# Four attention and feed-forward stages of a two-layer decoder in two barrier-free programs, and ALiBi's bias added by TensorE

## The chip, the cores and the metric

The kernel runs on one core of a Trainium2 chip. The metric is the device time of one execution in microseconds, as the median of several runs. TensorE, VectorE, ScalarE, GpSimd and SyncE are called PE, DVE, ACT, POOL and SP, as in the profile. Each engine works through its own instructions in order. They meet through semaphores: an instruction waits until a count is reached, and adds to another when it is done.

## The reference

The input x has 2048 tokens (32 sequences of 64) of 256 numbers, which is 16 tiles of 128 tokens. Six parts follow each other, each added to x, and each works on the layer norm of x:

```
x = x + attention(norm(x))            # 16 heads of 128, 4-bit weights with scales, softmax over 64 keys
x = x + cross_attention(norm(x), ctx) # 16 heads of 128, 4 key heads, RMS norm, rotary, 64 context + 64 causal keys
x = x + feed_forward(norm(x))         # silu(x Wg) * (x Wu), 2 of every 4 kept, then Wd
x = x + alibi_attention(norm(x))      # 16 heads of 16, 4 key heads
x = x + channel_attention(norm(x), ctx)
x = x + experts(norm(x))              # 32 experts, top 8
```

In the ALiBi attention the logits are `q k / 4 + slope * (key - query)`, and minus infinity where the key lies behind the query; then comes the softmax, the product with v and the output projection.

## The kernel before, in words

x stays in SBUF as 16 tiles of [128 tokens, 256]. A step is four tiles. The work is written as four stages. The first three are a block of five engine programs each (`with nc.Block()`), the fourth is made of three: ALiBi, channel attention and experts, which `together` (L131) writes one after the other into each engine's program without a barrier between them. `core.stage()` (L107) ends each stage with a barrier of all engines (L112).

**The first attention** (`attn_stage`, L299) goes through 64 units, one for each step and head. The loop over n = 0 to 68 (70 on DVE) is written out: PE takes the scores of unit n-1, the projections of unit n, the transposes and the mix of unit n-3 and the output projection of unit n-4. The last four units run out without new projections behind them. L572 adds the result to x, and `measure` (L209) takes the statistics of a tile.

**The cross attention** (`cross_stage`, L667) goes in 16 units a step (4 tiles, 4 key heads), with a lag for every operation (L698): tile s is normalised at t = 4s, turned at 2 units later (L776), projected from 4 later on (keys or values, then queries, into two PSUM banks), and the scores come 11 later. ACT squares what was projected, DVE multiplies it with the rotary tables (L950, L952, L953) and sums the squares (L970). The queries of a unit go to PE only when DVE has read the last ones. `settle` (L212) stands ahead of it: it aggregates the statistics of the tiles (L218) and takes the inverse root in twelve small dependent instructions (L197 to L203, one helper for all stages). `make_tables` makes the tables at t = 1.

**Feed-forward** (`ffn_stage`, L1083) has 32 units; the down projection follows nine units behind (FFN_LAG), so PE takes the last ones with nothing else to do. For a unit, DVE keeps two of four (L1167), ACT rounds to 16 bits (L1261), POOL takes the rest (L1113), and PE multiplies (L257). L1173 adds to x. SP has nothing to do in it.

**ALiBi** (`alibi_stage`, L1687) has two units a tile (`ALIBI_PAIRS`), with the lags of L1708: turn 1 (L1769), projection 2 (L257, 24 small matmuls; ACT copies q, v in four pieces, L1844, and k in eight, L1850), scores 4 (L1795), softmax sums 5, transposes of the probabilities and mix 7, output 8. For a unit's scores DVE does three things over [128, 512]: L1890 multiplies by the scale, adds the bias and writes to SBUF; L1894 takes the largest; L1896 subtracts it. The next scores wait for L1890, as there is one PSUM bank for them. DVE's rest of the projection's input (L1900) comes behind the odd unit's L1896, and PE's projection of the next tile waits for it. Ahead of it all, POOL sets the channel attention's buffers to constants (L1925, L1599 to L1603), DVE settles all 16 tiles and clears v (L1869).

`steps` (L235) writes the first, the last and the draining pass of a body out and runs those between in a register loop. The weights of each stage come by SP in turn with what POOL has split, during the stage ahead.

Of the kernel before, what the change touches and what calls it, by code (L numbers as in the profile page):

```python
# [47 lines left out]
AT_ATTN, AT_CROSS, AT_FFN = (26 * KB, 125 * KB), (56 * KB, 157 * KB), (56 * KB, 125 * KB)  # L48
# [67 lines left out]
class Programs:  # L116
# [7 lines left out]
    ahead: Any = None  # L124

# [109 lines left out]
def steps(engine, body, unrolled=0):  # L235

    body(0, lambda k: k >= 0)
# [33 lines left out]
ATTN_BLOCK = 32  # L273

# [24 lines left out]
def attn_stage(core, w, jobs=(), first=0):  # L299
# [3 lines left out]
    region = Region(core, AT_ATTN)  # L303
    sb = lambda shape, dt=F32: region.take(shape, dt)
    bias, bo = sb([P, 3, ATTN_HEADS]), sb([P, D])
    xT = [sb([P, STEPS, KD, TOK], F16) for p in range(2)]
    xnorm = sb([P, SUBS, D])
    codes, scales = (sb([P, ATTN_RAWS, CHUNK]) for _ in range(2))
    qT, kT = (sb([P, 2, TOK]) for _ in range(2))
    v = [sb([P, 2, SUBS, ATTN_GROUP * ATTN_HD], F16) for p in range(2)]  # L310
# [21 lines left out]
    LATE = 3  # L332

# [18 lines left out]
    with nc.Block() as block:  # L352
        @block.sync
        def _(sp):
            for j, (src, sc, dst) in enumerate(raw):
                if j >= ATTN_RAWS:
                    sp.wait_ge(s_made, j - ATTN_RAWS + 1)
                to, ts = (q[:, j % ATTN_RAWS, 0:int(np.prod(src.shape[1:]))] for q in (codes, scales))
                if len(src.shape) == 3:
                    to, ts = (q.rearrange("p (t d) -> p t d", d=D) for q in (to, ts))  # L360
                sp.dma_start(to, src).then_inc(s_raw[j % ATTN_RAWS], 16)
                for b in range(P // ATTN_BLOCK):
                    sp.dma_start(ts[b * ATTN_BLOCK:(b + 1) * ATTN_BLOCK], sc[b].partition_broadcast(ATTN_BLOCK)).then_inc(s_raw[j % ATTN_RAWS], 16)
            stage_weights(core, sp, jobs, first)

        @block.tensor
        def _(pe):
            def turn_x(tile, out):
                pe.wait_ge(s_normed, tile + 1)
                for k in range(KD):  # L370
                    last = nc.tensor.transpose(out[:, k].rearrange("p b c -> p (b c)"), xnorm[:, tile % SUBS, k * P:(k + 1) * P], core.ident)
                last.then_inc(s_turned, 1)

            def project_v(u):
                i, h = head(u)
                g, j, b = h // ATTN_GROUP, h % SUBS // 2, h % 2
                if i == 0 and h % ATTN_GROUP == 0:
                    pe.wait_ge(s_made, ATTN_PER_GROUP * g + 2)
                if h == 0:
                    pe.wait_ge(s_lo, SUBS * (i + 1))  # L380
                after(pe, q_kept, u)
                for k in range(KD):
                    tokens = [q[:, i, k, (2 * j + b) * P:(2 * j + b + 1) * P] for q in xT]
                    last = product(nc, ps[:, RING[3 * u % 2], :], tokens, [w.qkv[:, ATTN_V, k, g * ATTN_GROUP * ATTN_HD:(g + 1) * ATTN_GROUP * ATTN_HD]], k == 0, k == KD - 1)
                last.then_inc(v_ready, 1)

            def project_qk(u, c, bank, ready):
                i, h = head(u)
                if i == 0 and h % ATTN_GROUP == 0:
                    pe.wait_ge(s_made, ATTN_PER_GROUP * (h // ATTN_GROUP) + (4 if c == ATTN_Q else 6))  # L390
                for k in range(KD):
# [2097 lines left out]
```

## Time and profile before

| what | value |
|---|---|
| median of 3 runs | 1947.57 us (1943.87 to 1948.71) |
| the profiled execution's own time | 1948.45 us |
| its span, first to last instruction | 1946.7 us |
| mean granted TensorE clock | 0.962 of full speed |
| busy: PE, DVE, ACT, POOL | 87%, 78%, 53%, 37% |
| first attention | 0 to 359 us |
| cross attention | 360 to 843 us |
| feed-forward | 844 to 1007 us |
| ALiBi, up to its last addition to x | 1008 to 1182 us |
| channel attention and experts | to the end |

A line of the timeline gives the start, the time, the engine, the line of the kernel, the operation, the tiles and shapes, how many instructions were merged, and in brackets the idle time before it with what ended it. The granted clock is a share of TensorE's full 2.4 GHz; 0.5 is its lower level, 1.2 GHz.

### The profile page before, as it was taken

To read this page: it belongs to the slowest core of one execution; us is meant where nothing else is said; L and a number is where in the kernel's file an instruction comes from. 1 tells how busy PE (TensorE), PEld (TensorE's weight loads), DVE (VectorE), ACT (ScalarE), POOL (GpSimd) and SP (SyncE) were. 2 spreads that over 40 slices of the span, in tenths; PEclk is the share of its full clock that TensorE was granted. 3 is DMA by queue.
4 is the path that set the end of the run, shared out by engine and by line. 5 is a ranking of instruction groups with operands and counts; after the bars stand their busy time and mean duration, and the time that the engine had idled before them with its cause. 6 is when DMAs were issued, how large, how long until landed. Compare 5 with 4: busy or idle time off the path is not lost. (4 is left out here: it accounts for less than half of the span.)

```text
span 1946.7 us, 43266 instructions
## 1 busy us (share of the span) xinstructions
PE 1694.7 (87%) x15744; PEld 1000.1 (51%) x15744; DVE 1514.0 (78%) x2893; ACT 1031.5 (53%) x2056; POOL 716.1 (37%) x941
## 2 busy tenths in 40 slices
PE   5999999589999999979946775777777889999998
PEld 2656665357777677845533442222222346656565
DVE  5766666689989898859876989999999478666654
ACT  2666666245555555534415764888888533323222
POOL 4644321487767766503352343454441000000000
PEclk9999999889999999989977997999999999999999
DMA  9601000100000000000002111333331013212121
GB/s 241 176 24 53 26 13 2 56 20 12 12 10 11 10 8 4 2 1 1 1 9 49 41 36 37 88 96 92 95 85 40 23 62 100 84 59 81 63 82 49
DMA packets 87661, 94.90 MB, mean 49 GB/s; under 512 B 17568, under 2 KB 63264, under 8 KB 87456
## 3 DMA queue, kind: packets, MB, share of 16 engines
q1 hardware_dynamic: 83712, 87.76, 15.8%
q10 hardware_dynamic: 2976, 2.32, 0.5%
q8 instruction: 127, 2.08, 0.4%
q0 software_dynamic: 768, 2.10, 0.4%
q14 instruction: 78, 0.64, 0.1%
HBM read 78.51 MB, written 10.22 MB: 46 GB/s over the span
## 5 line engine op out<-in xcount | busy, mean ns | idle before, releaser
L257 PE MATMUL ps<-arena 128*128 128x512 f16 (+6 forms) x6464 | 1094.6, 325 | 57.4 <-DVE arena L1900 13.9
L257 PEld LDWEIGHTS ps<-arena 128*128 128x128 f16 (+1 forms) x6464 | 604.9, 100 | 446.9 <-issue 43.4
L1533 ACT ACTIVATE arena<-ps 128x512 f32<-128x512 f32 x512 | 278.6, 598 | 72.3 <-PE ps L1465 49.6
L1547 DVE TENSOR_REDUCE arena<-ps 128x4 f32<-128x1024 f32 x256 | 305.3, 1218 | 11.1 <-PE ps L1457 11.0
L1513 PE MATMUL ps<-arena 128*32 128x256 f32 x2048 | 164.2, 393 | 2.8 <-ACT arena L1542 0.6
L1457 PE MATMUL ps<-arena 31*128 31x256 f16 x1024 | 102.6, 276 | 73.2 <-ACT arena L1533 52.2
L2356 DVE TENSOR_TENSOR arena<-ps,arena 128x512 f32<-128x512 f32 x96 | 66.1, 689 | 128.2 <-ACT arena L2248 111.3
L2248 ACT ACTIVATE arena<-ps 128x512 f32<-128x512 f32 x96 | 57.1, 596 | 178.8 <-PE ps L257 178.6
L1457 PEld LDWEIGHTS ps<-arena 31*128 31x128 f16 x1024 | 34.8, 92 | 188.3 <-DVE arena L1547 153.2
L1020 POOL TENSOR_TENSOR arena<-arena 128x512 f32<-128x512 f32 x96 | 98.8, 1043 | 44.7 <-DVE arena L203 43.7
L623 POOL TENSOR_TENSOR arena<-arena 128x256 f32<-128x256 f32 x64 | 39.3, 614 | 188.6 <-DVE arena L593 188.6
L486 ACT ACTIVATE arena<-ps,arena 128x512 f32<-128x512 f32 x64 | 44.0, 688 | 115.2 <-PE ps L257 115.2
L1465 PE MATMUL ps<-arena 32*128 32x256 f16 x1024 | 101.2, 276 | 0.9 <-ACT arena L1533 0.2
L2238 ACT ACTIVATE arena<-arena 128x512 f16<-128x512 f32 x96 | 60.1, 626 | 74.2 <-DVE arena L2362 73.9
L1113 POOL TENSOR_TENSOR arena<-arena 128x512 f16<-128x512 f32 x32 | 50.2, 1577 | 115.7 <-ACT arena L1261 112.4
L179 POOL TENSOR_TENSOR arena<-arena 128x256 f16<-128x256 f32 (+5 forms) x72 | 86.1, 1196 | 5.8
L886 ACT ACTIVATE arena<-ps 128x512 f16<-128x512 f32 x64 | 38.2, 597 | 82.0 <-PE ps L812 82.0
L177 POOL CAST arena<-arena 128x256 f16<-128x256 f32 (+5 forms) x72 | 45.5, 632 | 97.2 <-DMA arena<-in_L_ffn_gate_up_proj 69.0
L1034 POOL TENSOR_TENSOR arena<-arena 128x256 f32<-128x256 f32 x80 | 58.3, 728 | 60.9 <-DVE arena L953 60.8
L1025 POOL TENSOR_TENSOR arena<-arena 128x512 f32<-128x512 f32 x64 | 67.2, 1051 | 28.0 <-DVE arena L988 27.8
L952 DVE TENSOR_TENSOR arena<-ps,arena 128x512 f32<-128x512 f32 x80 | 54.9, 686 | 28.7 <-ACT arena L881 25.8
L541 DVE TENSOR_TENSOR arena<-ps,arena 128x512 f16<-128x512 f32 x64 | 43.9, 686 | 40.5 <-ACT arena L475 40.5
(199 smaller groups left out, 2919.7 us busy)
## 6 DMA issues: line engine op xcount, KB each, us to landing
arena<-moe_cw SPq DMA_DIRECT2D x64, 192.0 KB, 2.7
arena<-moe_cw SPq DMA_DIRECT2D x64, 128.0 KB, 2.9
arena<-in_L_ffn_gate_up_proj SPq DMA_DIRECT2D x16, 384.0 KB, 3.4
ch_out<-arena SPq DMA_DIRECT2D x32, 128.0 KB
arena<-moe_cw SPq DMA_DIRECT2D x64, 64.0 KB, 2.7
ch_keys<-arena SPq DMA_DIRECT2D x48, 64.0 KB, 2.0
arena<-ch_keys SPq DMA_DIRECT2D x64, 48.0 KB
arena<-arena SPq DMA_DIRECT2D x192, 16.0 KB
```

Of the source, the lines that this page charges most:

```text
L179: nc.gpsimd.tensor_tensor(lo, raw, hi, ALU.subtract).then_inc(core.s_split, 1)
L257: last = nc.tensor.matmul(out, a, b, start=start and n == 0, stop=stop and n == len(pairs) - 1, skip_group_check=not group)
L1020: nc.gpsimd.tensor_tensor(a4, a4, spread(rms[:, s % 2, u * CROSS_KVH:(u + 1) * CROSS_KVH], CROSS_HD), ALU.mult).then_inc(scaled.sem, 1)
L1025: nc.gpsimd.tensor_tensor(prob[:, k % 2], e[:, k % 2], spread(inv[:, k % 2, :], CROSS_KEYS), ALU.mult).then_inc(probs.sem, 1)
L1034: nc.gpsimd.tensor_tensor(a4[:, :, 0:half], a4[:, :, 0:half], b4[:, :, half:CROSS_HD], ALU.add)
L1457: last = nc.tensor.matmul(ps[:, bank(user) + n, u * D:(u + 1) * D], qp[rows, tile % CH_RING, set8, u * P:(u + 1) * P], kp[rows, tile % CH_ ...
L1465: last = nc.tensor.matmul(ps[:, T[(t * CH_RGS + g) % len(T)], u * D:(u + 1) * D], kp[rows, tile % CH_RING, set8, u * P:(u + 1) * P], qp[ro ...
L1513: last = nc.tensor.matmul(ps[32 * g:32 * (g + 1), O, 0:D], vz[:, half % 2, u, g, j, :], pT[:, c % 3, g, u, :], start=j == 0 and u == 0, st ...
L1533: nc.scalar.activation(pT[:, b % 3, g], ps[:, T[n % len(T)], :].rearrange("p (u t) -> p u t", u=KD), ACT.Exp, scale=CH_SCALE).then_inc(s_e ...
L1547: nc.vector.tensor_reduce(m[:, half % 2, 2 * half_pair:2 * half_pair + 2, j, :], ps[:, bank(user):bank(user) + 2, :].rearrange("p g (u s) ...
L2238: nc.scalar.activation(hT[0][:, b % 4, :], h[b % MOE_HELD], ACT.Copy).then_inc(s_hi, 1)
L2356: nc.vector.tensor_tensor(h[n % MOE_HELD], ps[:, U[n % 2], :], silu[:, n % 2, :], ALU.mult).then_inc(s_gated, 1)
```

## The change

The four stages become two, each one program: both first attentions, and feed-forward to experts. The parts that change:

- The cross attention's first six units (t = 0 to 5) are issued by PE, ACT and DVE at the end of the first attention's n = 62 to 67; its POOL program starts behind the attention's own, and its first two context loads and all credits to semaphores are issued at the very start. DVE settles tiles 0 to 11 at n = 60, and 12 to 15 behind its last statistics. The buffers are placed anew so that both fit.
- ALiBi's first four units (t = 0 to 3) are issued in feed-forward's e = 37 to 40: on PE ahead of the down projection of e, on ACT ahead of e's roundings, on DVE at the end of e. DVE settles tiles 0 to 11 at e = 37, 12 to 15 at the end. PE's first mix waits for feed-forward's last addition. SP's ALiBi loads and POOL's preparations (`open_gpsimd`) come at feed-forward's start.
- ALiBi's bias, divided into three bf16 parts, is written into the scores' bank by three matmuls with the identity, and the scores are accumulated onto it. There are two banks for the scores; k and v share one. The scale goes into ACT's copy of q. L1890 is gone; L1894 and L1896 read PSUM. e lies where the logits are, so L1896 waits for the probabilities two units back.
- POOL's constants are set in pieces: the 8192 columns of L1925 in 8, one in each unit of the first step, the rest in 13 in the next two steps. The channel attention's keys are loaded at context tile 9, not 3.
- The channel attention's first turned scores also wait for ALiBi's last addition (`keys.accumulated`), at step 13, not 16.

```diff
-        with core.stage():
-            attn_stage(core, attn, later[0], first[0])
-        with core.stage():
-            cross_stage(core, cross, later[1], first[1])
-        with core.stage():
-            ffn_stage(core, ffn)
+            second = cross_stage(core, cross, later[1], first[1])
+            together(core, attn_stage(core, attn, second, later[0], first[0]), second)
...
+            last.append(ffn_stage(core, ffn, last[2]))
             together(core, *reversed(last))
...
+ATTN_CROSS = tuple(range(ATTN_UNITS - 2, ATTN_UNITS + 4))
+FFN_ALIBI = (37, 38, 39, 40)
...
+            if n in ATTN_CROSS:
+                ahead.tensor(pe, 0, ahead.begun, ATTN_CROSS.index(n), ATTN_CROSS.index(n) + 1)
...
+            if n == ATTN_CROSS[0] - 2:
+                settle(core, dve, "x_first", 0, range(TILES - SUBS))
+            if n in ATTN_CROSS:
+                ahead.vector(dve, 0, ahead.begun, ATTN_CROSS.index(n), ATTN_CROSS.index(n) + 1)
+        settle(core, dve, "x_last", 0, range(TILES - SUBS, TILES))
...
+            if e == FFN_ALIBI[0]:
+                settle(core, dve, "al_first", 2, range(TILES - SUBS))
+            if e in FFN_ALIBI:
+                ahead.vector(dve, 0, ahead.begun, FFN_ALIBI.index(e), FFN_ALIBI.index(e) + 1)
+        settle(core, dve, "al_last", 2, range(TILES - SUBS, TILES))
...
+                pe.wait_ge(s_bias, 2 * ALIBI_PARTS)
+                pe.wait_ge(shifted.sem, shifted.at(i, k - 1))
+                for n in range(ALIBI_PARTS):
+                    nc.tensor.matmul(ps[:, SC[k % 2], :].rearrange("p (r n) -> p r n", r=2), ident[:, :], parts[:, n, :].unsqueeze(1).broadcast_to([P, 2, ALIBI_KVH * S]),
+                                     start=n == 0, stop=False, skip_group_check=True)
                 for b in range(2):
-                        last = nc.tensor.matmul(ps[b * S:(b + 1) * S, SC, :], qT[:, s % 2, a, b * S:(b + 1) * S],
-                                                kT[:, s % 2, b].rearrange("p h k -> p (h k)"), start=True, stop=True)
+                    last = nc.tensor.matmul(ps[b * S:(b + 1) * S, SC[k % 2], :], qT[:, s % 2, a, b * S:(b + 1) * S],
+                                            kT[:, s % 2, b].rearrange("p h k -> p (h k)"), start=False, stop=True, skip_group_check=True)
...
-                    dve.wait_ge(exped.sem, exped.at(i, k - 1))
-                    nc.vector.scalar_tensor_tensor(out=lg.rearrange("p (r g) k -> p r (g k)", r=2), in0=ps[:, SC, :].rearrange("p (r n) -> p r n", r=2),
...
-                    nc.vector.tensor_reduce(top[:, k % 2, :], lg, AX.X, ALU.max).then_inc(maxed.sem, 1)
+                nc.vector.tensor_reduce(top[:, k % 2, :], sc, AX.X, ALU.max).then_inc(maxed.sem, 1)
                 dve.wait_ge(maxed.sem, maxed.at(i, k + 1))
-                    nc.vector.tensor_tensor(lg, lg, spread(top[:, k % 2, :], S), ALU.subtract).then_inc(shifted.sem, 1)
+                dve.wait_ge(probs.sem, probs.at(i, k - 1))
+                nc.vector.tensor_tensor(logits[:, k % 2], sc, spread(top[:, k % 2, :], S), ALU.subtract).then_inc(shifted.sem, 1)
...
+    def open_gpsimd(pool):
+        credit(pool, probs)
+        nc.gpsimd.memset(v, 0.0).then_inc(s_zero, 1)
+        pool.wait_ge(s_const, 16)
+        nc.gpsimd.tensor_copy(ident, core.ident).then_inc(s_bias, 1)
+        left = bias.rearrange("p g k -> p (g k)")
+        for n in range(ALIBI_PARTS):
+            nc.gpsimd.tensor_copy(parts[:, n, :], left).then_inc(s_bias, 1)
...
+                if i == 0:
+                    nc.gpsimd.memset(keys.rows[:, t // 2, t % 2 * CH_HALF:(t % 2 + 1) * CH_HALF], 1.0).then_inc(s_ones, 1)
+                if 1 <= i < STEPS - 1 and (i - 1) * ALIBI_UNITS + t < ALIBI_CLEARED:
+                    ahead.clear(pool, (i - 1) * ALIBI_UNITS + t)
```

## Rows read from the trace of the kernel before

**Rows 1.** The page: busy time and instructions of each engine

```profile
PE 1694.7 (87%) x15744; PEld 1000.1 (51%) x15744; DVE 1514.0 (78%) x2893; ACT 1031.5 (53%) x2056; POOL 716.1 (37%) x941
```

**Rows 2.** Busy time in four stretches (columns as in the first line, us)

```profile
core 0: us, PE busy (x) PEld busy (x) DVE busy (x) ACT busy (x) POOL busy (x), PEclk, DMA share, GB/s
0.00:50.00 50.00, 26.24 (x192) 11.50 (x192) 29.24 (x92) 15.80 (x30) 23.04 (x22) 0.97 0.99 242
...
345.00:386.60 41.60, 24.38 (x195) 12.25 (x195) 25.20 (x77) 11.52 (x21) 17.86 (x22) 0.84 0.19 58
...
997.41:1037.80 40.39, 14.93 (x105) 10.84 (x105) 19.90 (x42) 6.12 (x24) 17.77 (x14) 0.59 0.09 27
...
1147.47:1155.61 8.14, 6.17 (x81) 3.78 (x81) 7.50 (x17) 6.13 (x21) 3.27 (x5) 1.00 0.16 48
```

**Rows 3.** Timeline of ALiBi, one tile of its repeating part, PE and DVE (start us, us, ...)

```profile
1149.21 0.42 DVE L1900 TENSOR_TENSOR arena<-ps,arena 128x256 f16<-128x256 f32 x1
...
1149.69 1.35 PE L257 MATMUL ps<-arena 128*128 128x128 f16 x24 [0.59 <-DVE arena L1900]
...
1150.97 1.08 PE L1795 MATMUL ps<-arena 128*64 128x512 f32 x4
...
1152.10 0.69 DVE L1890 SCALAR_TENSOR_TENSOR arena<-ps,arena 128x512 f32<-128x512 f32 x1 [0.26 <-PE ps L1795]
...
1152.82 0.69 DVE L1894 TENSOR_REDUCE arena<-arena 128x8 f32<-128x512 f32 x1
...
1153.14 1.08 PE L1795 MATMUL ps<-arena 128*64 128x512 f32 x4
```

**Rows 4.** Timeline, ALiBi's first scores, and a weight load of the cross stage's first projection

```profile
370.46 0.15 PEld L257 LDWEIGHTS ps<-arena 128*128 128x128 f16 x1 [0.28 <-issue]
...
1035.89 1.98 PE L1795 MATMUL ps<-arena 128*64 128x512 f32 x4
```

**Rows 5.** Timeline of feed-forward, 24 matmuls of 512 columns, and its last units

```profile
866.66 5.34 PE L257 MATMUL ps<-arena 128*128 128x512 f16 x24
...
994.57 2.43 ACT L1261 ACTIVATE arena<-arena 128x512 f16<-128x512 f32 x4 [10.19 <-DVE arena L1167]
...
995.28 5.41 POOL L1113 TENSOR_TENSOR arena<-arena 128x512 f16<-128x512 f32 x4 [7.34 <-ACT arena L1261]
...
997.41 7.08 PE L257 MATMUL ps<-arena 128*128 128x256 f16 x48 [4.13 <-POOL arena L1113]
```

**Rows 6.** Timeline from feed-forward's last addition to ALiBi's third turn

```profile
1004.53 1.42 DVE L1173 TENSOR_TENSOR arena<-ps,arena 128x256 f32<-128x256 f32 x4 [7.85 <-PE ps L257]
...
1008.28 6.92 POOL L1925 MEMSET arena<- 128x8192 f16 x1 [7.59 <-POOLq L112]
...
1009.44 5.79 DVE L197 TENSOR_SCALAR arena<-arena 128x16 f32<-128x16 f32 x1
...
1030.57 2.18 ACT L1850 ACTIVATE arena<-ps,arena 128x128 f32<-128x128 f32 x8
...
1037.79 0.69 PE L1769 MATMUL ps<-arena 128*128 128x128 f32 x2
```

**Rows 7.** Timeline, first and last instruction of one settling of 8 tiles

```profile
1122.57 0.64 DVE L218 BATCH_NORM_AGGREGATE arena<-arena 128x2 f32<-128x6 f32 x8
...
1125.65 0.17 DVE L203 SCALAR_TENSOR_TENSOR arena<-arena 128x8 f32<-128x8 f32 x1
```

**Rows 8.** Timeline, from the first attention to the cross attention

```profile
329.07 0.42 DVE L578 TENSOR_TENSOR arena<-ps,arena 128x256 f16<-128x256 f32 x1 [1.07 <-ACT arena L491]
...
356.45 1.42 DVE L572 TENSOR_TENSOR arena<-ps,arena 128x256 f32<-128x256 f32 x4 [1.21 <-PE ps L257]
...
357.78 1.40 DVE L209 BATCH_NORM_STATS2 arena<-arena 128x6 f32<-128x256 f32 x4
...
366.00 0.69 PE L776 MATMUL ps<-arena 128*128 128x128 f32 x2 [9.66 <-DVE arena L226]
...
380.00 0.41 DVE L938 TENSOR_TENSOR arena<-ps,arena 128x256 f16<-128x256 f32 x1
```

More of the change, by code:

```diff
@@ L124 @@
     ahead: Any = None
+@dataclass
+class StageAhead:
+    open_tensor: Any
+    open_scalar: Any
+    open_vector: Any
+    open_gpsimd: Any
+    begun: Any
+    tensor: Any
+    scalar: Any
+    vector: Any
 def together(core, *stages):
@@ L332, in attn_stage @@
     LATE = 3
+    ahead = cross.ahead
     def late_tile(n):
@@ L350, in x_bank @@
         return ps[:, (*RING, SC, T)[tile], 0:D].rearrange("p (k b c) -> p k b c", k=KD, b=2)
[L352 to L374, printed above, removed]
@@ L375, in project_v @@
                 i, h = head(u)
-                g, j, b = h // ATTN_GROUP, h % SUBS // 2, h % 2
+                pe.wait_ge(o_lo, u + 1)
+                if h == 0:
+                    after(pe, added, SUBS * i)
                 if i == 0 and h % ATTN_GROUP == 0:
[L378 to L391, printed above, removed]
-                    last = product(nc, ps[:, bank, :], [w.qkv[:, c, k, h * ATTN_HD:(h + 1) * ATTN_HD]], [q[:, i, k, :] for q in xT], k == 0, k == KD - 1)
-                last.then_inc(ready, 1)
@@ new lines, in tensor @@
+                    pe.wait_ge(s_made, ATTN_PER_GROUP * (h // ATTN_GROUP + 1))
+                for s in range(SUBS):
+                    last = product(nc, ps[:, A[s // 2], s % 2 * D:(s % 2 + 1) * D], [q[:, u % 2, (s % 2 * 2 + s // 2) * P:(s % 2 * 2 + s // 2 + 1) * P] for q in oT],
+                                   [w.out[:, h, :]], h == 0 and s % 2 == 0, h == ATTN_HEADS - 1, group=False)
+                last.then_inc(projected, 1)
+            if n in ATTN_CROSS:
+                ahead.tensor(pe, 0, ahead.begun, ATTN_CROSS.index(n), ATTN_CROSS.index(n) + 1)
@@ new lines, in cross_stage, with sb @@
+    homes = {"in": Region(core, AT_CROSS_IN), "early": Region(core, AT_CROSS_EARLY), "rope": Region(core, AT_CROSS_ROPE),
+             "late": Region(core, AT_CROSS_LATE), "last": Region(core, AT_CROSS_LAST)}
+    home = {"cRaw": "in", "raw": "in", "maskf": "in", "ropeA": "rope", "v": "late", "kT": "late", "shift": "last", "prob": "late", "pT": "early", "qT": "early", "top": "last"}
+    def sb(name, shape, dt):
+        return homes[home.get(name, "early")].take(shape, dt)
+    xT = [sb(f"xT{p}", [P, 2, KD, P], F16) for p in range(2)]
@@ L1923, in gpsimd @@
     def gpsimd(pool):
-        credit(pool, probs)
-        nc.gpsimd.memset(keys.rows, 1.0).then_inc(s_ones, 1)
-        ahead.clear(pool)
         def split_context(n):
```

1815 lines of the change are left out of this document (932 added, 883 removed).

## The prediction

> **What bounds the kernel now.** I read the page first: PE is busy for 87% of the span and DVE for 78% [rows 1]. Both are averages over stages with other limits, so I then went through windows of 50 us, and through the timeline of the three places that the change touches. Three things are to be seen.
>
> At the two joints nobody is near its limit. From feed-forward's last down projections to the turn of ALiBi's third tile pass 40.4 us, with PE busy for 14.9 and DVE for 19.9, at a granted clock of 0.59 [rows 2]. Most of DVE's share isn't work: a settling instruction of 16 columns takes 5.79 us while POOL fills 8192 columns in 6.92 us [rows 6], where such an instruction takes 0.17 us alone [rows 7]. From the first attention's tail to the end of the cross attention's first tile pass 41.6 us, with DVE busy for 25.2 [rows 2].
>
> ALiBi in its repeating part takes 8.14 us a tile, with DVE busy for 7.50, PE for 6.17 and ACT for 6.13 [rows 2]. What closes the loop is a chain: the projection's input is ready (L1900, 1149.63), PE projects and scores until 1152.05, DVE goes through L1890, L1894, L1896 and the rest until the next L1900 has ended, 5.67 us later at 1149.63 + 8.14 [rows 2, 3].
>
> The rest (attention, cross, feed-forward, channel, experts) keeps its instructions and order, and I give it no change beyond what is named below.
>
> **ALiBi's bias.** L1890 goes, which is 0.72 us from its start to that of L1894 [rows 3], twice a tile. L1894 and L1896 stay; reading PSUM I leave them at 0.69 us, as L1890 reads it too and takes 0.69. PE gets three matmuls of 512 columns a unit. 24 such take 5.34 us, so one is 0.22 and three are 0.66 us, 1.3 us a tile, if the clock is high [rows 5]; at the low clock a weight load with its idle time, one for each matmul, has 0.43 us [rows 4].
>
> Now the chain: the even unit's three stand between projection and scores, so PE's part grows from 2.47 to 3.1 us. DVE's part of 5.67 us loses both L1890, 1.44 us. That would be 7.35 us. But the odd unit's scores, which ended 2.17 us after the even ones (1154.22 against 1152.05 [rows 3]), now end 2.8 us after them, and DVE without one L1890 would be there about 0.4 us too early. That gives 7.7 us a tile, and PE's own work, 6.17 + 1.3 = 7.5 us, lies just under it. So about 0.45 us is saved a tile, for 13 tiles 6 us. The last tiles have no projection, and there DVE is the limit: two of them save 1.44 less what PE asks, some 2 us together. I take **-8 us**. At best DVE's whole 1.44 us is saved for 15 tiles, -22 us; at worst PE takes all back, 0. Beyond 0 I don't go at the high clock, since the chain holds both edits. The new wait of L1896 for the probabilities two units back has POOL's product as its source, which ends about as L1896 would start; I give it nothing, and what stands behind it is DVE's whole queue, so up to 0.2 us a unit, 6 us, if POOL is late.
>
> **From feed-forward to ALiBi.** Gone: the barrier, the long settling, the constants ahead of everything. Before, the last addition starts at 1004.53 and the third tile's turn at 1037.79 [rows 6]. After, I follow the tail. DVE settles twelve tiles as soon as it has kept the last units. Eight tiles take 1125.82 - 1122.57 = 3.25 us, 0.64 of it for the eight aggregations [rows 7], so twelve take 3.6 and four take 2.9. It has kept the last unit shortly before ACT's last rounding ends at 997.0 [rows 5]; the settling is done at about 1000.4, and the first tile is normalised at 1000.9. PE finished unit 28 at 999.2 (a quarter of 7.08 us from 997.41 [rows 5]) and now waits 2.3 us, with three down projections behind it. ACT is worse off: it turns the first input, and then stands before q, v and k of tile 0 (k alone is 2.18 us [rows 6], the three about 3.4), all ahead of the last rounding. PE projects at about 1003.3 to 1005.5, so that rounding comes at 1009, POOL's rest (1.35 us each [rows 5]) at 1010.6, and the last down projection ends at 1012.5 and not at 1004.5. This is the price of the moved steps: 8 us later. Then come the addition and the statistics, 2.8 us, the last settling, 2.9, and a normalisation, 0.4: 1018.7. The third tile's turn is at about **1019, and not at 1037.8: -19 us**. PE has fewer gaps on the way, so I expect the high clock earlier; ALiBi's first scores took 1.98 us and not 1.08 [rows 3, 4]. I give this 2 us: **-21**. At best the tail isn't held up at all: 1004.5 + 2.8 + 2.9 + 0.4 = 1010.6, -27. At worst the moved PE and ACT steps take the low clock and their waits add, another 8 us: -12.
>
> **From first to cross attention.** Before, the moved chain of six steps runs from the first turn, 366.00, to 380.00, 14.0 us. The attention's tail from 345.0 to its addition at 356.45 is 11.5 us [rows 8]. Both are latency chains. They could overlap, but each queue holds them in one order: DVE's rope products of tile 0 stand in front of the last unit's rounding, for which PE waits with the last output projection, and behind that PE projects for step 5. So I lay them end to end. Added is the settling of twelve tiles at n = 60: 3.6 us in DVE's queue, where PE waits for L578 in every unit and DVE has 1.07 us idle ahead of it [rows 8]; PE loses 2.3 us. Then addition and statistics, 2.8, and the last settling, 2.9. 345.0 + 11.5 + 14.0 + 2.3 + 2.8 + 2.9 = 378.5, where before it was 380.0. PE and ACT run on during the last settling, and this closes some of DVE's waits in steps 6 and 7. I take **-2 us**. At best DVE stands idle nowhere from 345 to 386.6, which saves 41.6 - 25.2 = 16.4 less 2.3 and 2.9, -11. At worst the tables and the turn's round trip aren't hidden either, +6.
>
> **Small ones.** The two context loads now leave at the start, where the DMA engines are busy for 0.99 of 50 us at 242 GB/s [rows 2]: 0.26 MB are 1.1 us, and PE waits for weights there: **+1** (0 to +2). POOL's preparations for the bias run during feed-forward's first settling: seven small instructions, of which DVE may wait for some, **+1** (0 to +3). The 21 pieces of the constants in ALiBi's steps, 6.92 / 8 = 0.87 us each for the larger, can hold DVE's normalisation, once a tile; it has about 0.4 us of slack there, **+1** (0 to +6). The held instruction of [rows 6] is what I go by. The Trainium skill's page "SBUF — State Buffer", section "Who interferes with whom", says that DVE and GpSimd share one port pair as an exclusive lock held for a whole instruction, and that copies, casts and `tensor_scalar` of DVE may need it, but `tensor_reduce` never. The trace agrees: L197 lasts as long as the fill lasts. By that rule alone each of the seven normalisations beside the larger pieces could lose up to 0.87 us, and no other DVE instruction in ALiBi's loop anything; the sum would be at most 6 us higher. SP's ALiBi loads come earlier and wait for nothing that is needed; the key loads, later by six tiles, still have 60 us.
>
> **Sum.** -8 - 21 - 2 + 1 + 1 + 1 = -28 us. The profiled execution took 1948.45 us, its span 1946.7; the median is 1947.57, 0.9 lower. So 1920.5 for the one and 1919.5 for the median.
>
> **The rivals.**
> - *The joints pay, the bias doesn't*: PE becomes ALiBi's limit and its waits for ACT stay. For it: PE at 7.5 us against 8.14, ACT at 6.13. Then -20: 1927.5. Chance 0.15.
> - *The tails overlap well*: at both joints DVE finds its data ready, -9 and -6 more: 1904.5. For it: DVE's idle 16.4 us at the first joint; against it the fixed order of the queues. Chance 0.12.
> - *ALiBi is bound by DVE alone*: the odd scores are ready in time and 1.44 us is saved a tile, -12 more: 1907.5. Against it stands PE's sum of 7.5 us. Chance 0.08.
> - *TensorE's clock falls in ALiBi* (slower): its mean was 0.59 around the joint [rows 2]. At 1.2 GHz PE needs nearly twice 7.5 us a tile, 14.9, and not 8.14; over 13 tiles that costs 88 us against 20 that the joints give: about 2015. It decides from 3 tiles of 13 at the low level, 6.8 us each. For it: ALiBi begins cold; against it: PE has fewer gaps than before. The Trainium skill's page "TensorE: Matmul & The Clock Gate" calls the low clock the default and says that activity releases it; by that rule more matmuls help, and this rival is less likely. Chance 0.04.
> - *It doesn't do what it says*: the moved steps wait where they stand and the tails lose what the barriers gave: no change, 1945. Chance 0.03.
>
> The forecast has 0.58. A measurement of this kernel can tell about 0.3%, 6 us. **Faster 0.92, same 0.03, slower 0.05.** The range takes in the joints' and ALiBi's bounds without all of them meeting: **1903 to 1934**.
>
> **What would show it.** ALiBi's additions (before at L1917) 7.6 to 7.8 us apart in the repeating part; 8.1 would mean PE took all, 6.8 that DVE binds. ALiBi's third turn within 15 us of the end of the last down projection, and that end some 8 us later than before when counted from the last keep. The cross attention's second turn no earlier than before by more than a few us. The settling at n = 60 as a gap of about 2 us in PE. Wrong would be a low clock through ALiBi, or a tail of feed-forward held by more than 12 us.

## The result, and the profile after

The changed kernel takes **1912.62 us** (median of 4 runs, 1911.80 to 1919.4) against 1947.56 for the kernel before in the same comparison: ratio 0.983, 95% interval 0.9815 to 0.9845, 35 us less. The forecast was 1919.5, with a range of 1903 to 1934. The profiled execution's own time is 1911.81 us, its span 1910.0 (before 1946.7).

The page of the changed kernel, its busy time, to be set against [rows 1]:

```profile
PE 1707.1 (89%) x15840; PEld 1004.0 (53%) x15840; DVE 1489.9 (78%) x2884; ACT 1031.2 (54%) x2056; POOL 720.3 (38%) x965
```

PE has 96 matmuls more, three for each of ALiBi's 32 units. At 0.22 us each they are 21 us, yet PE is busy for only 12.4 us more: the rest of its work took 9 us less, at a mean granted clock of 0.975 where it was 0.962. DVE has 24 us less; 22 of them are the bias (32 units of 0.69 us). The page doesn't say where the 36.7 us of the span went. For that I put the same marks of both traces side by side (us; the ALiBi marks are its first and last addition, at L1917 before and at L1976 after):

```
mark                                     before     after    so far
attention's unit with scores near 340    341.28    339.96     -1.3
cross attention's third turn             398.59    397.63     -1.0
cross attention's last addition          841.93    838.99     -2.9
feed-forward's first normalisation       847.61    846.77     -0.8
ALiBi's third turn                      1037.79   1019.37    -18.4
ALiBi's first addition                  1062.32   1039.54    -22.8
ALiBi's last addition                   1181.64   1148.71    -32.9
end of the span                         1946.7    1910.0     -36.7
```

So the joint of feed-forward and ALiBi gives 22 us from feed-forward's start to ALiBi's first addition, and ALiBi itself 10.

The second joint in the timeline of the changed kernel (start us, duration us, engine, line, count, idle time before it and what ended it), which answers to [rows 5, 6]:

```profile
996.77 2.38 PE L275 MATMUL ps<-arena 128*128 128x256 f16 x12 [4.00 <-POOL arena L1147]
1000.62 0.69 PE L1829 MATMUL ps<-arena 128*128 128x128 f32 x2 [1.46 <-DVE arena L244]
1001.10 5.39 PE L275 MATMUL ps<-arena 128*128 128x256 f16 x48
1010.07 4.28 PE L275 MATMUL ps<-arena 128*128 128x256 f16 x36 [3.36 <-POOL arena L1147]
...
1006.09 2.18 ACT L1917 ACTIVATE arena<-ps,arena 128x128 f32<-128x128 f32 x8
1008.11 0.68 ACT L1304 ACTIVATE arena<-arena 128x512 f16<-128x512 f32 x1
...
1012.15 1.42 DVE L1207 TENSOR_TENSOR arena<-ps,arena 128x256 f32<-128x256 f32 x4 [2.63 <-PE ps L275]
...
1019.37 0.44 PE L1829 MATMUL ps<-arena 128*128 128x128 f32 x2 [3.34 <-DVE arena L244]
```

The tail is held where the prediction put it: ACT makes eight key copies of ALiBi's first tile (L1917) and only then the last rounding (L1304), PE waits 3.36 us for what POOL makes of it, and the last addition starts at 1012.15 (forecast: last down projection ends at 1012.5; before 1004.53). Then 7.2 us to the third turn at 1019.37 (forecast 1019).

Windows of the changed kernel (length, busy us of each engine, granted clock, DMA share, GB/s), from its last down projections but three to the third turn, and one repeating tile of ALiBi, against [rows 2]:

```profile
996.77:1019.37 22.60, 14.43 (x108) 10.54 (x108) 11.25 (x46) 9.72 (x31) 9.86 (x12) 0.77 0.09 25
1047.23:1054.91 7.68, 7.46 (x89) 4.19 (x87) 6.45 (x15) 6.12 (x21) 4.08 (x6) 1.00 0.15 43
```

A tile takes 7.68 us in place of 8.14, with PE busy for 7.46 of them; DVE has fallen from 7.50 to 6.45.

### The profile page after: what moved, and what is told of

It reads as the page before. It is cut to its first block, busy times and chain, and to the rows that moved or that the text cites. A ratio compares the mean times of both kernels' runs of the same rounds, so it can differ in the third digit from the quotient of the medians.

```text
span 1910.0 us, 43448 instructions
## 1 busy us (share of the span) xinstructions
PE 1707.1 (89%) x15840; PEld 1004.0 (53%) x15840; DVE 1489.9 (78%) x2884; ACT 1031.2 (54%) x2056; POOL 720.3 (38%) x965
## 4 chain that ended last, share of the span: by engine, by line
DVE 23%; PE 22%; issue 6%; POOL 3%; ACT 1%; DVEq 0%; POOLq 0%; ACTq 0%
PE ps L275 18%; DVE arena L1592 14%; POOL arena L1147 2%; PE ps L1859 1%; PE ps L1502 1%; PE ps L1856 1%; DVE arena L2440 1%; DVE arena L2436 0%; DVE arena L1201 0%; DVE arena L244 0%; POOL arena L2013 0%; DVE arena L2371 0%; DVE arena L2369 0%; DVE arena L1952 0%; ACT arena L2312 0%
## 5 line engine op out<-in xcount | busy, mean ns | idle before, releaser
L275 PE MATMUL ps<-arena 128*128 128x512 f16 (+6 forms) x6464 | 1090.9, 324 | 54.6 <-POOL arena L1147 9.6
L652 POOL TENSOR_TENSOR arena<-arena 128x256 f32<-128x256 f32 x64 | 39.5, 617 | 180.4 <-DVE arena L617 180.4
```

The lines of the kernel that those rows point to most:

```text
L275: last = nc.tensor.matmul(out, a, b, start=start and n == 0, stop=stop and n == len(pairs) - 1, skip_group_check=not group)
```

## The experiments

Twelve experiments ran, the first of them the changed kernel once more. "The changed kernel" in a comparison is this repeat or the result above. Its two medians lie 4.3 us apart, and its single executions spread from 1907.90 to 1919.86 us, so I read distances inside a trace first and medians second. Each kernel has one trace, the changed kernel two.

### The changed kernel once more

> The changed kernel once more, to see how far one profiled execution of it lies from another. Theory (the tail of the first attention met a colder clock in the first trace): from the attention unit whose scores start near 340 us to the cross attention's third turn pass 54.5 us, as in the traces of the experiments with the same first joint, where the first trace of the changed kernel has 57.7; median 1911 to 1915 us. Rival (the longer tail is the kernel's own): 57.7 again.

No edit. 1916.92 us, ratio 0.9825 (0.9794 to 0.9855); both forecasts of this run missed, the median of 1911 to 1915 too. From the attention unit's scores (341.23) to the third turn (398.96) it is 57.7 us again, as the rival had it. Yet of the experiments below with the same code at the first joint, four have 54.4 to 54.6 us. The windows show a difference in the clock: here 350 to 360 us in the repeat, in the first trace of the changed kernel, and in "no step ahead at the second joint" (54.6 us).

```profile
350.00:360.00 10.00, 7.57 (x75) 5.12 (x74) 2.91 (x6) 2.52 (x5) 5.05 (x6) 0.50 0.23 67
```

```profile
350.00:360.00 10.00, 7.65 (x74) 4.92 (x75) 2.85 (x6) 2.23 (x5) 3.91 (x3) 0.56 0.22 67
```

```profile
350.00:360.00 10.00, 6.32 (x83) 3.88 (x81) 4.37 (x8) 3.61 (x7) 4.90 (x5) 1.00 0.21 67
```

The granted clock is 0.50 and 0.56 (nearly all at the level of 1.2 GHz) in two executions and 1.00 (2.4 GHz) in the third, in the gaps of the attention's tail, with the same instructions. The nine traces with this code fall into two groups: four with the low clock there and 57.7 or 57.8 us, five with the high one and 54.4 to 55.7, so the low clock goes with some 3.2 us more. Whether the execution decides this or the kernel isn't shown at this place, since both traces of the changed kernel have the low clock and no kernel was traced at both levels. Behind ALiBi's third turn it is shown for one kernel: from that turn to the first addition pass 20.17 us at a clock of 1.00 in the first trace and 23.67 at 0.80 in the repeat. Together the two places are worth 6.7 us.

### The bias back on VectorE

```diff
-                for n in range(ALIBI_PARTS):
-                    nc.tensor.matmul(...)
+                nc.vector.scalar_tensor_tensor(out=lg, in0=ps[:, SC[k % 2], :], scalar=1.0, in1=bias, op0=ALU.mult, op1=ALU.add)
```

> The changed kernel with ALiBi's bias added on VectorE again, as one more instruction a unit; the second bank for scores, the joint programs and the moved steps stay. Theory (the bias's move pays): ALiBi's additions, 7.68 us apart in the changed kernel, go back to 8.1 us apart; 13 tiles and the last ones make +8 to +10 us, about 1921. Rival (the second bank for scores did it, not the move): the distance stays at or under 7.75 us and the time within 2 us of 1912.6.

1944.07 us, ratio 0.9981: nearly the whole gain is gone, and both theories missed by over 20 us. A tile takes 9.14 us. DVE's timeline has the reason:

```profile
1060.80 0.69 DVE L1951 SCALAR_TENSOR_TENSOR arena<-ps,arena 128x512 f32<-128x512 f32 x1 [0.90 <-POOL arena L2008]
1061.53 0.69 DVE L1955 TENSOR_REDUCE arena<-arena 128x8 f32<-128x512 f32 x1
1062.25 0.69 DVE L1957 TENSOR_TENSOR arena<-arena 128x512 f32<-128x512 f32 x1
```

In the changed kernel the exponentials lie in place of the logits. My edit wrote the logits with its first instruction, so the wait for POOL's product of two units back stood ahead of three instructions and not of the last. The second form of this experiment gives the exponentials their own array again and waits as before the change:

```diff
-    e = logits
+    e = sb("e", [P, 2, 8, S], F32)
-                dve.wait_ge(probs.sem, probs.at(i, k - 1))
+                dve.wait_ge(exped.sem, exped.at(i, k - 1))
```

> The changed kernel with the bias on VectorE again, but the exponentials in an array of their own, as before the change: VectorE's first instruction of a unit waits for the exponential two units back, not for GpSimd's product. Theory (the earlier experiment's 9.14 us a tile came from that wait for the product, now ahead of three VectorE instructions): the additions come 8.0 to 8.2 us apart and the time is 1921 to 1925. Rival one (the second bank for scores gives the gain): 7.8 us apart or less, time under 1917. Rival two (something else costs 9.14): still over 8.8, 1938 or more.

1931.35 us, ratio 0.991 (0.9894 to 0.9927). The additions in the repeating part are 8.14 us apart, as they were before: with the bias on VectorE the second bank for scores gives nothing there, and the bias's move gives 0.45 us a tile. (The bias on TensorE with one bank wasn't tried.) But the whole costs 14.4 us against the repeat and lies above the 1921 to 1925 us that I expected. From first to last addition it is 122.15 us against 108.63. The difference, 13.5, is 0.45 for each of six quiet tiles (2.7), 3.5 at the last four, and 7.3 on the five tiles at the turns of the stage's loop, every fourth, one of them with the settling: 9.24, 8.57, 9.26, 11.56 and 9.88 us, where the repeat has 7.80, 7.77, 7.69, 10.29 and 7.68. The kernel before takes 119.32 us from first to last addition, 2.8 less than this one at the same quiet distance; what these 2.8 are is open, and so is whether all of the 13.5 would be the bias's in the old kernel.

### One, two and three parts, and one f32 matmul

```diff
-ALIBI_PARTS = 3
+ALIBI_PARTS = 1
```

> The changed kernel with the bias in one bf16 part in place of three: two of TensorE's three bias matmuls a unit are left out, and with them the bias's lower 16 bits of mantissa. Theory (TensorE's work is what ALiBi's loop now waits for, 7.4 us busy of 7.68): the additions come 7.1 to 7.3 us apart, DVE with 6.45 us of work not yet binding; 5 to 7 us less in all, about 1906.5. Rival (the chain through VectorE, ScalarE and GpSimd binds): the distance stays above 7.6 and the time within 1.5 us of 1912.6.

1906.96 us, ratio 0.9792; the distance is 7.17 us, as expected. So PE's work is what the loop waits for with three parts. The other way round, a dearer bias:

```diff
-                for n in range(ALIBI_PARTS):
-                    nc.tensor.matmul(..., ident[:, :], parts[:, n, :]..., start=n == 0, stop=False)
+                nc.tensor.matmul(..., core.ident, bias..., start=True, stop=False)
```

> The changed kernel with the bias as one f32 matmul of 512 columns a unit in place of three bf16 ones, the identity in f32 as weights. Two f32 matmuls of 512 columns, in four instructions, are 1.08 us in the trace, so one would be 0.54 against 0.66 to 0.75 for the three. Theory (TensorE's work sets ALiBi's distance, and an f32 matmul costs what the scores' do): 7.3 to 7.5 us a tile, 3 to 5 us less in all. Rival (with all 128 rows of weights, or a broadcast operand, it costs twice that): 8.3 us a tile or more, 9 us slower.

1919.82 us, ratio 0.9855. The f32 matmul is two instructions of 0.5 us, 1.02 to 1.10 us with its weights:

```profile
1083.32 1.02 PE L1855 MATMUL ps<-arena 128*128 128x512 f32 x2
1084.27 1.08 PE L1858 MATMUL ps<-arena 128*64 128x512 f32 x4
```

The rival was right in kind: one matmul costs what I had taken for two. The scores' have 64 columns of weights and this one has 128; whether that is the reason wasn't tried. A tile takes 8.19 us. PE's busy time a tile, with one part, with three and with the f32 matmul (one window of each kernel):

```profile
1053.40:1060.58 7.18, 6.49 (x85) 3.81 (x82) 6.35 (x15) 6.00 (x21) 4.08 (x6) 1.00 0.17 48
```

```profile
1079.85:1088.05 8.20, 7.90 (x88) 4.29 (x85) 6.45 (x15) 6.12 (x21) 3.82 (x9) 1.00 0.54 97
```

From three parts to the f32 matmul PE gains 0.44 us of work and the tile 0.51: there PE sets the pace. From one part to three it gains 1.0 and the tile 0.51. I take it that below three parts the chain through DVE is nearly as long, with half of PE's added work, the even unit's, in it; this is argued from the sums and no experiment takes that chain apart.

### No step ahead at the second joint

```diff
-FFN_ALIBI = (37, 38, 39, 40)
-ALIBI_AHEAD = 4
+FFN_ALIBI = ()
+ALIBI_AHEAD = 0
```

(and one settling of 16 tiles at the end in place of two)

> The changed kernel with no step of ALiBi inside feed-forward: one program still, all 16 tiles settled at feed-forward's end, then ALiBi from its first step. Theory (the barrier and the constants were most of the joint, the steps bring less): the last down projection ends at about 1004 us and not at 1012; addition and statistics 2.8, settling 3.7, normalisation 0.4, then 12 us from first to third turn: third turn at about 1023, where the changed kernel has 1019.4; with up to 4 us of a colder clock behind it the time is 4 to 8 us above 1912.6, about 1919. Rival one (the steps are most of the gain): 12 us or more above, 1925 or later. Rival two (the held tail eats what the steps give): within 2 us of 1912.6.

1918.59 us, ratio 0.9857. The timeline of PE (the last down projections, then the first, second and third turn):

```profile
994.81 7.38 PE L275 MATMUL ps<-arena 128*128 128x256 f16 x48 [5.56 <-POOL arena L1147]
1009.17 0.69 PE L1827 MATMUL ps<-arena 128*128 128x128 f32 x2 [6.98 <-DVE arena L244]
1013.02 0.67 PE L1827 MATMUL ps<-arena 128*128 128x128 f32 x2
...
1022.62 0.48 PE L1827 MATMUL ps<-arena 128*128 128x128 f32 x2
```

Counted from the cross attention's last addition (841.93, 836.76, 838.99), the third turn comes after 195.9 us before, 185.9 here and 180.4 in the changed kernel. So the one program and the constants' new places give 10.0 (net of 2.1 that feed-forward's start loses, below), the steps ahead 5.5.

Which of those two it is can be read from the settling. The kernel before (first four lines) and this one (last three):

```profile
1009.44 5.79 DVE L197 TENSOR_SCALAR arena<-arena 128x16 f32<-128x16 f32 x1
1015.27 3.44 DVE L198 TENSOR_SCALAR arena<-arena 128x16 int32<-128x16 int32 x1
1018.74 1.74 DVE L199 TENSOR_SCALAR arena<-arena 128x16 int32<-128x16 int32 x1
1025.14 0.41 DVE L226 TENSOR_SCALAR arena<-arena 128x256 f32<-128x256 f32 x1 [0.18 <-DVEq L1872]
...
1004.99 1.17 DVE L236 BATCH_NORM_AGGREGATE arena<-arena 128x2 f32<-128x6 f32 x16
1006.19 0.18 DVE L215 TENSOR_SCALAR arena<-arena 128x16 f32<-128x16 f32 x1
1008.70 0.41 DVE L244 TENSOR_SCALAR arena<-arena 128x256 f32<-128x256 f32 x1
```

From the first aggregation to the first normalisation it is 16.90 us before (from 1008.24) and 3.71 here, 13.2 less. Before, three settling instructions lasted 5.79, 3.44 and 1.74 us, each to the end of one of POOL's fills (6.92, 3.54 and 1.82 us). That is 10.4 of the 13.2 us; 1.7 are the clearing of v (L1869) with its waits, and the rest small instructions beside other work of POOL's. The barrier ahead of the settling shows as 0.98 us of DVE's idle time, 0.04 here. So most of this joint's gain is that DVE no longer settles beside the constants, and about 1 us is the barrier; 4.1 of the sum is lost again at feed-forward's start, in feed-forward and between the first and third turn (13.45 us here, 12.19 before). No run moves the constants alone, with the four stages left as they were.

### No step ahead at the first joint

```diff
-ATTN_CROSS = tuple(range(ATTN_UNITS - 2, ATTN_UNITS + 4))
+ATTN_CROSS = ()
```

> The changed kernel with no step of the cross attention inside the first attention: one program, all 16 tiles settled at its end, then the cross attention from its first step. Theory (laid end to end, the overlap gives back in the tail what it takes from the head): last addition of the attention back at about 356 us, first turn at about 363.5, second turn's split at about 377.5, where the changed kernel has 378.9; time 1 to 2 us below 1912.6, about 1911. Rival (the steps hide work): second turn's split at 384 or later, time 1917 or more.

1917.54 us, ratio 0.9838 (0.9816 to 0.9859), no different from the changed kernel. Its last addition is at 355.61 and its second turn's split at 376.11, near the 356 and 377.5 expected; from the unit's scores (340.44) to the third turn (394.46) it is 54.0 us. The changed kernel's code has 54.5 at the high clock and 57.7 at the low one, the kernel before 57.3. The six steps ahead hide nothing here; what the first joint gains, 3 us, comes with the one program, and four of the nine traces with this joint lose it again at the low clock. Nor is that the whole price of the steps. They need the early settling at n = 60, which lies ahead of the unit that I count from. In the changed kernel one unit's scores come 6.67 us behind the last ones there, and PE waits:

```profile
328.32 0.69 PE L429 MATMUL ps<-arena 128*64 128x64 f32 x16
333.56 0.52 PE L463 MATMUL ps<-arena 64*128 64x64 f16 x24 [1.63 <-DVE arena L602]
334.99 0.69 PE L429 MATMUL ps<-arena 128*64 128x64 f32 x16
```

In this kernel all units are 4.97 us apart. So the steps ahead cost 1.7 us more, 2.2 in all at the high clock. The median, 1917.54, is what the rival had named (1917 or more) and lies above the 1911 us that I expected; but the repeat of the changed kernel has 1916.92, and the split is 8 us ahead of the rival's 384.

### Two orders mended

In feed-forward's tail, ScalarE's rounding goes first:

```diff
-            if e in FFN_ALIBI:
-                ahead.scalar(act, 0, ahead.begun, ...)
             if 1 <= e <= FFN_UNITS:
...
                 nc.scalar.activation(hT[0][:, k % FFN_MEMBERS], ..., ACT.Copy).then_inc(s_hi, 1)
+            if e in FFN_ALIBI:
+                ahead.scalar(act, 0, ahead.begun, ...)
```

> The changed kernel with one order turned round: on ScalarE each of feed-forward's last roundings goes ahead of ALiBi's copies of the same round, not behind them. Theory (the copies hold the last rounding, and it the last down projection): that projection follows without the 3.4 us wait, the last addition starts 3.4 us earlier after the last keep, the third turn too; time 3 us under the changed kernel's in the same comparison. Rival (the projections of ALiBi's first tile on TensorE hold it, not ScalarE's order): within 1 us.

1913.03 us, ratio 0.9822 (0.9804 to 0.9839). In its timeline the last 12 down matmuls follow the second turn without a wait:

```profile
1004.07 0.62 ACT L1302 ACTIVATE arena<-arena 128x512 f16<-128x512 f32 x1
...
1009.94 0.38 PE L1829 MATMUL ps<-arena 128*128 128x128 f32 x2
1010.16 1.47 PE L275 MATMUL ps<-arena 128*128 128x256 f16 x12
...
1018.32 0.44 PE L1829 MATMUL ps<-arena 128*128 128x128 f32 x2 [2.87 <-DVE arena L244]
```

First to third turn is 15.25 us, against 18.75 and 18.76 in the two traces of the changed kernel: 3.5 less, as expected. The median, 3.9 below the repeat and 0.4 above the first result, can't show it. The distance by itself can't either: "GpSimd's preparation later", below, keeps the old order and has 15.81 us. There the old wait stands as before, 3.36 us, but the clock is at 1.00 for the seven us behind the first turn, where the two traces of the changed kernel have 0.76 and 0.69 and this one 0.58:

```profile
1003.22 3.96 PE L275 MATMUL ps<-arena 128*128 128x256 f16 x48
1010.76 2.66 PE L275 MATMUL ps<-arena 128*128 128x256 f16 x36 [3.36 <-POOL arena L1148]
```

So what the experiment shows is the wait: 3.35 to 3.37 us in every kernel with the steps ahead in the old order, none here.

In the attention's tail, the cross attention's last two steps go one round later:

```diff
-ATTN_CROSS = tuple(range(ATTN_UNITS - 2, ATTN_UNITS + 4))
+ATTN_CROSS = (62, 63, 64, 65, 67, 68)
```

> The changed kernel with the cross attention's fifth and sixth step one round later: VectorE rounds the attention's last output ahead of them, and TensorE projects it ahead of them. Theory (the moved steps hold the attention's tail for as long as they gain at the head): the last addition starts at about 361 us in place of 371 to 373, the settling ends 10 us earlier, and the third turn comes 2 us earlier counted from the last full attention unit; time 2 us lower. Rival (the cross attention's own chain binds): third turn and time 0 to 3 us later, since its projections start later.

1908.59 us, ratio 0.9794 (0.9778 to 0.9811), 8 us under the repeat. In the changed kernel (first trace) DVE stands in the cross attention's products, L979 to L999, before it rounds the attention's last output, L581, for which PE waits with the last projection:

```profile
360.50 0.69 DVE L979 TENSOR_TENSOR arena<-ps,arena 128x512 f32<-128x512 f32 x1 [4.82 <-ACT arena L902]
...
364.19 0.74 DVE L581 SCALAR_TENSOR_TENSOR arena<-ps,arena 128x512 f16<-128x512 f32 x1
...
364.98 5.32 PE L275 MATMUL ps<-arena 128*128 128x256 bf16 x20 [3.85 <-DVE arena L581]
380.58 6.82 PE L275 MATMUL ps<-arena 128*128 128x512 f16 x18 [5.50 <-DVE arena L982]
...
373.36 1.40 DVE L596 TENSOR_TENSOR arena<-ps,arena 128x256 f32<-128x256 f32 x4
```

With the two steps later:

```profile
357.80 0.75 DVE L581 SCALAR_TENSOR_TENSOR arena<-ps,arena 128x512 f16<-128x512 f32 x1 [1.34 <-ACT arena L533]
...
358.61 5.23 PE L275 MATMUL ps<-arena 128*128 128x256 bf16 x26 [0.59 <-DVE arena L581]
...
365.30 1.41 DVE L596 TENSOR_TENSOR arena<-ps,arena 128x256 f32<-128x256 f32 x4
...
369.26 5.75 PE L275 MATMUL ps<-arena 128*128 128x512 f16 x18 [3.32 <-DVE arena L982]
```

PE's waits of 3.85 and 5.50 us (the same in "no step ahead at the second joint", at the high clock) become 0.59 and 3.32, and from the unit's scores to the third turn it is 49.1 us at the high clock (54.5 for the changed kernel's code): 5.4 less, where I had expected 2. With the 1.7 us of the early settling, the steps ahead now gain 3.2 us against no steps at all (54.0). The profiled execution of the repeat had the low clock there, which is another 3.2 us.

Both together:

> The changed kernel with both orders mended: ScalarE's last roundings of feed-forward ahead of ALiBi's copies, and the cross attention's fifth and sixth step one round later. Theory (each tail was held by its own queue, and the two don't touch): the gains add, 4 and 8 us, so 12 us under the changed kernel, 1903 to 1907 us, ratio to the kernel before 0.978. Rival (what is gained early is lost at the next wait, or the lower clock takes it): 1909 or more, no better than the better one of the two alone.

1908.67 us (1902.31 to 1908.78), ratio 0.9786 (0.9767 to 0.9806). In the trace both distances are shorter: 51.7 us from scores to third turn with a clock of 0.55 from 350 to 360 us (57.7 less 6.0), and 14.15 us from ALiBi's first to its third turn. From the attention unit's scores to ALiBi's last addition it is 804.1 us, where the edits alone have 806.6 (first joint) and 809.2 (second), and the changed kernel 808.8 and 814.3 in its two traces. That is 10.2 less than the repeat but only 4.7 less than the first trace, which had the high clock behind ALiBi's third turn (20.17 us, here 23.65 at 0.80). The median, 8 us under the repeat and 4 under the first result, is that of the first-joint edit alone, as the rival had it: each gain is seen in its own place, and that they add up in the whole isn't shown.

### GpSimd's preparation later, and a last combination

```diff
     def gpsimd(pool):
-        ahead.open_gpsimd(pool)
         for k in range(FFN_UNITS):
+            if k == FFN_MEMBERS:
+                ahead.open_gpsimd(pool)
```

> The changed kernel with GpSimd's preparation of ALiBi's bias and values moved behind feed-forward's fourth rest, so that it no longer runs beside feed-forward's first settling. Theory (GpSimd's instructions held VectorE's): the settling of 16 tiles, from its first aggregation to the first normalisation 4.75 us in the changed kernel and 3.72 before it, is back at 3.7; 1 us less in the trace, too little for the median. Rival (the settling is longer for another cause): it stays at 4.7.

1914.36 us, ratio 0.9834. Feed-forward's first settling takes 3.71 us again (843.30 to 847.01). In the changed kernel it takes 4.75. Two of its instructions, 16 columns each, with the GpSimd instruction beside the first:

```profile
844.03 0.69 POOL L1993 TENSOR_TENSOR arena<-arena 128x256 f32<-128x256 f32 x1
844.23 0.53 DVE L220 TENSOR_TENSOR arena<-arena 128x16 f32<-128x16 f32 x1
845.29 0.17 DVE L220 TENSOR_TENSOR arena<-arena 128x16 f32<-128x16 f32 x1
```

The second L220 began 0.02 us ahead of GpSimd's next product (845.31) and took 0.17 us; with GpSimd's preparation later all three L220 take 0.17 or 0.18. The other microsecond stays: between the cross attention's statistics and the settling lie 2.03 us in both, and 0.96 before. The Trainium skill's page "SBUF — State Buffer", section "Who interferes with whom", also says that a DVE instruction with two SBUF inputs contends with a GpSimd instruction that reads SBUF; the first L220 agrees, with 0.53 us beside such a read, against 0.17 where none was running.

The last kernel has both orders mended, this edit, and two parts of the bias:

> The changed kernel with both orders mended as in the experiment before, GpSimd's preparation behind feed-forward's fourth rest, and the bias in two bf16 parts (the third, its lowest 8 bits of mantissa, is left out). Theory (each bias matmul counts in full in ALiBi's distance: 7.68 us with three, 7.17 with one): 7.42 us a tile; with 13 such tiles 3.5 us less than with three parts, so 1903 to 1906 us. Rival (two parts already meet the chain through the other engines): 7.17 to 7.2 us, and 1900 to 1903.

1903.63 us (5 runs, 1903.18 to 1908.65), ratio 0.9775 (0.9759 to 0.979): 45 us under the kernel before, and the fastest. A tile takes 7.39 us, with PE busy for 7.03, where the theory had 7.42: the third part is worth 0.29 us a tile, the second 0.22.

```profile
1068.78:1076.17 7.39, 7.03 (x87) 4.00 (x85) 6.45 (x15) 6.00 (x21) 3.81 (x9) 1.00 0.59 125
```

## Why the prediction was right, point by point

**The second joint, -21.** Measured -21.9, from feed-forward's first normalisation to ALiBi's first addition (-17.5 in the repeat), and its inner steps to half a microsecond on the trace's clock: tail at 1012.15 for 1012.5, third turn at 1019.37 for 1019. Counted from feed-forward's start, which came 0.8 us earlier, the third turn gained 17.6 and not 19; behind it 4.4 came and not 2. The price of the moved steps, 8 us, was real, and the wait of 3.4 us in it was only ScalarE's order, as the experiment shows. The long settling was rightly named as the thing to get rid of, and it is most of the gain (10.4 us in three instructions, against about 1 for the barrier). The 2 us for the clock were right in sign, but it is a matter of the execution: 4.4 in the first trace (24.53 us before against 20.17), 0.9 in the repeat.

**The first joint, -2.** In the first trace the settling ends at 378.87 for 378.5, and the second turn's split is at 378.90. That this fits to 0.4 us is luck. Tail and chain lie end to end, because of DVE's order, as the later-steps experiment confirms: from the unit's scores to the end of the settling the forecast has 34.9 us, and at the high clock it is 35.6. But in that trace it is 38.9, since I took the tail at the clock of the trace before, where it is 0.96 from 350 to 360 us, and in both traces of the changed kernel it is 0.50 to 0.56. And the unit's scores start at 339.96 and not at 343.6: the attention ahead of it came 3.0 us earlier, and the settling at n = 60 cost 1.7 us where 2.3 were forecast. The two errors, 4.0 late and 3.6 early, cancel. With the settling's 1.7 us, the joint measured -1.1 at the high clock and +2.1 at the low.

**ALiBi's bias, -8.** The distance was forecast at 7.7 and is 7.68, PE's busy time at 7.5 and is 7.46. (The rows give 2.42 and 5.72 us for the two parts of the chain, where the prediction has 2.47 and 5.67; the sum is the same.) The term was mis-sized: from first to last addition 10.2 us are gained in the first trace, 10.7 in the repeat, and 13.5 against the bias put back. The step that fell short is "about 0.45 us is saved a tile, for 13 tiles 6 us". It read the quiet tiles alone. Before, five tiles are longer than 8.14 by 0.3 to 3.4 us (8.46, 8.85, 9.27, 11.54 and 9.42), at the turns of the stage's loop and its settling; in the repeat the same five cost 6.3 us less and not 2.3. That the bias's move brings this is shown by putting it back (7.3 us on the same five). DVE has 1.2 us to spare in a tile now, so what delays it would be absorbed; that this is the mechanism is argued from the windows, not shown by an experiment of its own. The other end of the step, L1896's new wait for POOL, was right at nothing (0.7 us in all), and the first bias experiment shows what it would cost one place earlier: 1.0 us a tile.

**The small ones.** POOL's preparation +1: measured +1.03, and shown. Start DMA +1: the scores of the unit ahead of the early settling start between 328.2 and 331.4 us over the executions, at 331.35 before: no loss that can be seen. The pieces of the constants +1: one normalisation took 1.89 us beside a product and a piece of POOL's, the others at most 0.7; nothing of it shows in the distances of 7.68, but that one stands ahead of the first addition, and what it costs there isn't known. Not foreseen were 1.07 us more at the entry of the second program, and 3.8 us less between ALiBi's end and the end, in code that the change hardly touches. Over the traces of all these kernels that stretch has 761 to 767 us, before it has 765.0; but the changed kernel's two have 761.3 and 761.8. Whether this is spread between executions or a small gain is open.

**Sum.** -22.8 up to ALiBi's first addition, where -21 was forecast (the joints, the start's loads, POOL's preparation), -10.2 in ALiBi for -7, and -3.8 behind it for 0. Of the 8.7 us between forecast and the first trace's span, 3.2 are ALiBi's under-sized term, 1.8 lie ahead of ALiBi, and 3.8 in a stretch that stays open; the repeat's trace is 7.4 us longer than the first one, as much as most of this. The rival "the tails overlap well" was not what happened: the tails were held as forecast. The rival "the bias doesn't pay" is refuted by its distance, "bound by DVE alone" by one part against three, and the slower one, a low clock through ALiBi, by the window at 1.00; its kin is real, though, in single stretches of 10 us.

## What to carry to other kernels

When steps of the next stage are put among the last of the one ahead, go through each queue of each engine and ask which instruction of the old stage now stands behind one of the new: here two such places cost 3.5 and 5.4 us and each was mended by moving a line or two. At the first joint the moved steps hid nothing until that was done, and cost 2 us. And look at what runs beside the small instructions at a joint before you blame the barrier: at the second joint three settling instructions beside large fills held 10.4 us, the barrier about one. When an engine at its limit is relieved, don't count the quiet rounds alone: here the five disturbed ones gave 5.8 to 6.3 us and the six quiet ones 2.7.

## What was not expected of the hardware

TensorE's granted clock behind a gap isn't settled by the kernel alone: the stretch behind ALiBi's third turn ran at 1.00 in one execution of the changed kernel and at 0.80 in another, 3.5 us apart. In the attention's tail, 350 to 360 us, it was 0.50 and 0.56 in these two and 1.00 in a kernel with the same instructions there, 3.2 us apart. An f32 matmul with 128 columns of weights and 512 moving ones took 1.02 to 1.10 us, more than three bf16 ones together (0.81).
